# A graph network's first stage: each gather of Q rows waits for the K and V tile of its number

## What is computed

```python
x = _layernorm(x + _L0_gnn_ref(x, src, dst, ...))        # attention over edges, 8 heads
x = _layernorm(x + _L1_gnn_ref(x, W_lin, W_attn, a, src, dst))   # graph attention, 4 heads
x = _layernorm(x + _L2_gnn_ref(x, src, dst, ...))        # 5 layers of neighbour sums and two matmuls
x = _layernorm(x + _L3_gnn_ref(x, edge_index, ...))      # 3 layers of neighbour means and two matmuls
```

```python
Q = (text_emb @ Wq.T + bq).reshape(N, H, DK)
K = (text_emb @ Wk.T + bk).reshape(N, H, DK)
V = (x @ Wv.T + bv).reshape(N, H, DK)
scores = jnp.sum(Q[col] * (K[row] + rel), axis=-1) / sqrt(DK)
```

## Time and profile before

| | us |
|---|---|
| median of three runs | 2918.83 |
| the three runs | 2916.10, 2918.83, 2921.84 |
| span of the profiled execution | 3243.1 |
| first stage in the profile, to the next stage's first gather | 165.95 |
| first Q gather starts | 87.71 |
| last Q gather starts | 123.28 |
| last K and V add starts | 161.02 |

### The profile page before, as it was taken

One profiled execution on the slowest core, in us unless ns is written; L12 is line 12 of the kernel. 1 busy time (PEld: TensorE's weight loads), 2 busy tenths in 40 slices (PEclk: granted clock), 3 DMA queues, 4 the chain that ended last, 5 costly groups with the idle time before them and its releaser, 6 DMA issues. The chain is left out here.

```text
span 3243.1 us, 53070 instructions
## 1 busy us (share of the span) xinstructions
PE 2724.4 (84%) x17114; PEld 1944.9 (60%) x17114; DVE 1576.1 (49%) x2779; ACT 1084.9 (33%) x3016; POOL 969.2 (30%) x1020
## 2 busy tenths in 40 slices
PE   6748888888861777777776999999999998999998
PEld 4637777777741666666663555555555656565665
DVE  8357777777653767666757224141514224111123
ACT  1014444444430556555562222040404034111111
POOL 2346666666335556565634001010101000000000
PEclk7869999999985899999996999999999999999999
DMA  6568888888333476666664433424252514444433
GB/s 246 174 191 266 254 262 252 257 254 258 109 93 70 88 122 131 121 124 121 122 101 154 142 102 120 135 90 130 80 149 69 150 37 138 124 118 115 127 106 96
DMA packets 332504, 470.20 MB, mean 145 GB/s; under 512 B 155942, under 2 KB 243062, under 8 KB 331588
## 3 DMA queue, kind: packets, MB, share of 16 engines
q1 hardware_dynamic: 269364, 286.33, 33.0%
q0 software_dynamic: 59088, 176.67, 18.9%
q10 hardware_dynamic: 3776, 3.80, 0.4%
HBM read 412.95 MB, written 55.50 MB: 144 GB/s over the span
## 5 line engine op out<-in xcount | busy, mean ns | idle before, releaser
L827 POOL DMA_INDIRECT e_from_src<-vk,src x416 | 393.9, 947 | 302.5 <-PE e_part_ps L1019 161.0
L827 POOL DMA_INDIRECT e_from_src<-val,src x416 | 394.1, 947 | 276.5 <-PE e_part_ps L1019 129.1
L2321 PE MATMUL sum_ps<-room,high 128*128 128x391 f16 x1900 | 470.3, 331 | 2.4 <-DVE z_t L2498 2.4
L2321 PE MATMUL sum_ps<-room,low 128*128 128x391 f16 x1824 | 454.0, 331 | 0.0
L2719 PE MATMUL sum_ps<-room,high 128*128 128x391 f16 x1200 | 389.4, 329 | 0.5 <-DVE x L2863 0.5
L1017 PE MATMUL e_part_ps<-e_onehot,e_from_src 128*128 128x129 f32 x1664 | 304.2, 309 | 96.4 <-issue 51.7
L2719 PE MATMUL sum_ps<-room,low 128*128 128x391 f16 x1152 | 379.3, 329 | 0.0
L1017 PEld LDWEIGHTS e_part_ps<-e_onehot,e_from_src 128*128 128x128 f32 x1664 | 241.2, 208 | 125.7 <-issue 69.6
L1121 ACT ACTIVATE sums<-e_part_ps 128x384 f32 x416 | 205.2, 493 | 328.6 <-PE e_part_ps L1019 234.0
L1017 PE MATMUL e_part_ps<-x,e_from_src 128*128 128x129 f32 x1664 | 273.2, 287 | 36.0 <-issue 24.7
L897 DVE TENSOR_TENSOR e_from_src<-e_from_src,e_fixed 128x2048 f32<-128x2048 f32 x104 | 237.5, 2284 | 113.2 <-ACT e_fixed L1102 70.7
(11 more groups left out here) (421 smaller groups left out, 4418.3 us busy)
## 6 DMA issues: line engine op xcount, KB each, us to landing
room<-adj SPq DMA_DIRECT2D x128, 977.5 KB, 4.9
e_window<-q_part SPq DMA_DIRECT2D x416, 128.0 KB
room<-adj SPq DMA_DIRECT2D x32, 488.8 KB
room<-adj SPq DMA_DIRECT2D x32, 391.0 KB
adj<-e_counts SPq DMA_DIRECT2D x8, 1250.0 KB
adj<-e_counts SPq DMA_DIRECT2D x8, 1193.8 KB
e_from_src<-vk,src POOLq DMA_INDIRECT x416
e_from_src<-val,src POOLq DMA_INDIRECT x416
```

The costliest lines, as they stand in the source:

```text
L827: nc.gpsimd.indirect_dma_start(from_src[:, b, j, :], None, by_src, bass.IndirectOffsetOnAxis(ap=keep["src"][:, g * G + j:g * G + j + 1], a ...
L2321: mm = nc.tensor.matmul(sum_ps[KH * n + m][:, 0:AN], part[:, t, m * P:(m + 1) * P], slab[s][:, n, k * AN:(k + 1) * AN], start=(t == 0 and ...
```

## The change

Ahead of each of the 29 gathers POOL waits until the K and V tile of the same number has been added; the last four, which have no such tile, wait for the 25th like gather 24.

```diff
@@ -303,6 +303,7 @@
                 pool.wait_ge(q_rows_out[i], 16 * len(range(i, NT, OB)))
             for i, (lo, hi) in enumerate(PIECES):
                 for t in range(lo, hi):
+                    pool.wait_ge(kv_made, min(t + 1, NT))
                     nc.gpsimd.indirect_dma_start(q_parts[:, t, :], None, scratch["q"],
                                                  bass.IndirectOffsetOnAxis(ap=keep["part_node"][:, t:t + 1], axis=0)).then_inc(staged[i], 16)
```

## The result

| | before | after |
|---|---|---|
| median, us | 2917.56 (10 runs, 2911.26 to 2921.84) | 2926.29 (10 runs, 2922.60 to 2937.46) |
| ratio after to before | | 1.0035, interval 1.0022 to 1.0048 |
| span of the profiled execution, us | 3243.1, later 2928.3 and 2919.8 | 2924.4 |

The kernel became 0.35% slower, +10.2 us by the ratio (6.4 to 14.0 by its interval); the two medians lie 8.7 us apart. The forecast was +9.7, 2928 us.

The account below looks back on a forecast made before the run. The K and V line was taken to end the first stage; waits 0, first 24 gathers 0, tail +9.7 us and no gain from the crawl gave 2918.8 + 9.7 = 2928 us, range 2905 to 2933.

Parts of the forecast that it names:

- What bounds the stage: First stage: the K and V line ends it, last add ending at 161.71 us, with the gathers long over.
- The 29 waits: POOL, ahead of each gather: nothing to 0.30 us each, up to 7.2 us uncovered; taken as 0.
- The gathers of tiles 0 to 23: POOL's first 24 gathers start later, following their tiles; no cost while K and V are last.
- the crawl: First stage, slow K and V adds around tiles 5 to 7 in the first profile: costs 24.4 us there.
- The tail: Gathers 24 to 28 behind the 25th add: 11.5 us to the last landing, new cost 9.7, up to 11.3.
- the landing: Last gather's start to ACT's issue of the last piece: 3.4 us with queues nearly empty, far end 4.8.
- s = 0: Share of the K and V slowdown that unprofiled runs have and the change removes: taken near 0, break-even 0.40.
- Rivals 1 and 2: K and V slowdown real: pacing removes it, -14.7 us, 2904, chance 0.26; or half, about 2919 us, chance 0.26.
- rival 3: K and V slowdown follows the paced gathers: +9.7 or tens of us more; little chance, within the forecast's 0.48.
- rival 4: POOL's waits never bind because K and V run ahead of the gathers; excluded.
- The sign that was set for the crawl: Adds of tiles 4 to 8 at 1.7 to 2 us after the change would show dependence on the gathers' pace.
- The even share of 28.9 us: First stage's 17.4% part of the profile's extra 324.3 us, spread evenly over the 1863 us outside the graph layers.

Follow-up runs that it names:

- before's second profile: The kernel before, unchanged (the added wait taken out), profiled again after the first profile of 3243.1 us; span 2928.3 us.
- the third profile: The kernel before, unchanged, profiled once more together with the last three variants; span 2919.8 us.

## Why the prediction came out

**What bounds the stage.** Right in its conclusion. The stage ends at the later of two lines: the last K and V add with its store and the barrier, 4.2 us; or the last gather's start with its landing (3.9 to 7.5 us in these traces), the last piece (3.3 to 4.9) and the barrier (about 2). Before, the second line had little to spare. In before's second profile the last piece was issued at 125.97 and landed 4.3 us later, at 130.3, while SP, which had issued its last store by 85.34 + 45.46 = 130.80, saw it land at 132.4: 2.1 us. In the third profile it is 1.4 us. After, the second line is the one that ends the stage. The rows of before's second profile, from the timeline, the list of SP's waits, and the issues with their median time to landing:

```profile
85.34 45.46 SPq L252 DMA_DIRECT2D vk<-pr_kv_out  x25
...
125.97 0.40 ACTq L586 DMA_DIRECT2D q_part<-pr_part_room  x1
...
SPq L254 <- DMA vk<-pr_kv_out: 1.6, 1, 1.6
...
q_part<-pr_part_room ACTq DMA_DIRECT2D x1, 640.0 KB, 4.3
```

The same rows correct a small term: from the last add's end to the last store's landing 2.0 us pass, not the 1.8 that the working subtracted, since the store's own issue lies ahead of SP's wait of 1.6.

**The 29 waits.** Taken at nothing, measured at no more than 0.013 us each where the tile is already there.

**The gathers of tiles 0 to 23.** "No cost" was right in after only because the last five come later still. As a separate statement it was too generous: pacing even to the fifth tile uses up the slack of some 2 us, which the first profile could not show, since there the crawl had put the K and V line's end 30 us behind that of the gathers' line (161.71 against 131.2 at the latest).

**The tail.** The working gave some 14 us from the add to the next stage, and 16.57 were measured, over the mark of 16 that I had set for it. Its terms:

| term | predicted, us | measured in after, us |
|---|---|---|
| add's end to gather 24's start | 0 | 0.27 |
| four gaps | 5.0 | 5.00 |
| last gather's start to issue of the last piece | 3.4, far end 4.8 | 5.97 |
| last piece and barrier | 3.1 + 2.4 | 3.3 + 2.0 |

The term that was mis-sized is the landing. The step behind it said that the queues are nearly empty once K and V are done. They are not: the same wait that holds the last five gathers holds gather 23 as well, and so the third piece's 1 MB lies in the queue beside them. The variant that delays only the last five shows the term with empty queues, 3.86 us, and the variant with the last nine shows both in one trace: gathers land in 2.8 us ahead of the third piece and in 4.8 beside it. Nor need it be that piece: with the wait on the tile four before, SP's K and V stores ran beside the last gather instead, and it took 5.90 us. Thus the trace's loss is 16.57 - 4.24 = 12.3 us where 9.7 was forecast; the timed +10.2 (6.4 to 14.0) holds both and can't choose. That the forecast met the timed figure to 0.5 us is luck within that interval.

**The crawl.** s = 0 was right: paced, late or free gathers leave the K and V line at 45.75 to 45.83 us. Rivals 1 and 2 fall by that for executions such as the timed ones, rival 3 by after's own adds, 1.73 us apart, and rival 4 by the 20 gathers that waited. The sign that was set for the crawl misled: adds of tiles 4 to 8 at an ordinary pace in after were to mean that it hung on the gathers' pace, and before's second profile has the same adds with the gathers unpaced. The Trainium skill, "SBUF — State Buffer", section "Who interferes with whom", says that a DMA never contends with a compute engine. The rows agree: the K and V line takes 45.83 us at a DMA share of 0.90 and 45.75 at 0.77.

**The reason for s = 0** was half wrong. The prediction said that the profiler had stretched the non-dense 1863 us, and that a run without it has no crawl. The profiler does not do that: two more profiled executions of the same kernel span 2928.3 and 2919.8. It was that one execution. The even share of 28.9 us for the first stage was near what the comparison gives, 165.95 - 134.69 = 31.3 us (32.9 against the third profile); the crawl's 24.4 was near what the K and V line had more there, 161.71 - 90.06 - 45.83 = 25.8 us. The doubt put against it, that the two edge stages might hold most of the extra time, was well founded. The first one's 416 gathers ran from 166.0 to 819.8, 654 us, and 519 us in the second profile, their 1.25 us apiece; the second one's took 662 us and 533. That is 264 of the 315 us by which the two profiles differ.

```profile
L827 POOL DMA_INDIRECT e_from_src<-vk,src x416: 942/947/956, 134.7 to 654.0; - x139
```

The best reading would have been the plain one: a span 11% above the median isn't the execution being predicted, and its long unexplained waits should be left out of the sum, as was done, without giving the profiler for their cause. The right s thus rested in part on a wrong reason.

## What to carry to other kernels

A wait that ties a second line of work to the pace of the line that ends the stage costs its own tail: what is left to do behind the last release, here four gaps, one landing and one store, and it is to be counted with whatever else the same wait has pushed into that window. It gains only if the paced work was taking something from the bounding line; here the bounding engine's busy share (38.76 of 40 us) said that it was not, while the busy DMA engines (0.90) alone would have suggested that it was. A profile whose span is far from the median should be taken again before anything in it is explained.

## What the runs showed of the hardware

In before's second profile 16 DMA engines were busy for 0.90 of 40 us and moved 306 GB/s, and the K and V line of TensorE and VectorE lost no pace by it (45.83 us, against 45.75 in after at 0.77 and 258 GB/s). What suffered was the DMAs themselves: the same 128 KB gather landed after 2.7 us at the least and 7.5 at the most in that profile, with a median of 4.6. In after, with less traffic, these were 2.9, 6.0 and 4.1. The last gather landed after 3.8 us with no other queue at work (only the last five wait), and after 5.9 beside ACT's piece (after) or SP's stores (four tiles before).

What slowed the execution of 3243.1 us stays open. In it, VectorE's adds came up to 16.9 us after the modelled end of the sums they read the earlier trace rows, with no releaser, at a granted clock of 0.75 over the stretch, where before's second profile and after have 1.00. None of the nine other profiled executions shows it, so it couldn't be put to a test.
